# The first calls of the work beside a second alignment moved ahead: two before its second step, one past its fifth

## The reference

```python
x = x + _L0_xattn_ref(ctx_1024, _layernorm(x, axis=-1))   # an alignment (DTW) of 64 latents to 1601 rows
x = x + _L0_attn_ref(_layernorm(x, axis=-1), ...)         # a gated linear recurrence, 64 steps
x = x + _L0_ffn_ref(_layernorm(x, axis=-1), ...)          # 8 experts, top 2, and a shared one
```

```python
r = d_ij + jnp.minimum(jnp.minimum(up, left), diag)        # the table
...
choice = jnp.argmin(jnp.stack([cd, cu, cl]))               # the path, from its end
...
expanded = jnp.zeros((T_large, d), dtype=small.dtype).at[j_idx].add(contrib)
```

## Time and profile before

| | |
|---|---|
| median of three runs | 1174.21 us |
| the profiled execution | 1176.61 us |
| its span, first to last instruction | 1175.4 us |
| mean granted TensorE clock | 0.938 of full |
| busy: PE, DVE, ACT, POOL | 86%, 56%, 42%, 10% |
| chain that ended last: PE, DVE, DMA | 55%, 29%, 6% |

### The profile page before, as it was taken

The page is one execution under the profiler, slowest core; times in us unless marked ns, Lnnn a source line. Parts: engine busy times, 40 slices in busy tenths (PEclk is TensorE's granted clock), DMA queues, the critical chain, the costliest instruction groups (busy, mean ns, idle before and its releaser), DMA issues.

```text
span 1175.4 us, 15523 instructions
## 1 busy us (share of the span) xinstructions
PE 1005.5 (86%) x4892; PEld 598.2 (51%) x4892; DVE 660.5 (56%) x2311; ACT 494.2 (42%) x847; POOL 115.5 (10%) x150
## 2 busy tenths in 40 slices
PE   5886639888891799997899699887999999999998
PEld 2332213333330455553576465645676767676776
DVE  4994949999999776487669612427311111111116
ACT  4885627766781345423242155243222222222221
POOL 1000000000000000000000000000252425242210
PEclk9998979999996799988899799799999999999999
DMA  9999954565876989440050097394121212123115
GB/s 354 324 309 272 274 155 141 154 190 157 237 225 163 327 252 329 135 150 11 1 186 1 0 336 249 104 349 174 49 83 57 83 56 84 56 84 105 32 52 182
DMA packets 123806, 190.47 MB, mean 162 GB/s; under 512 B 9008, under 2 KB 93136, under 8 KB 123728
## 3 DMA queue, kind: packets, MB, share of 16 engines
q1 hardware_dynamic: 117840, 171.13, 47.0%
q0 software_dynamic: 5888, 18.36, 5.1%
HBM read 165.43 MB, written 24.03 MB: 161 GB/s over the span
## 4 chain that ended last, share of the span: by engine, by line
PE 55%; DVE 29%; DMA 6%; issue 4%; ACT 3%; SPq 2%; POOL 0%; DVEq 0%; ACTq 0%; POOLq 0%
PE bank L1816 13%; PE bank L1663 8%; PE bank L1847 7%; PE bank L1684 4%; DVE table L825 4%; PE bank L1808 3%; DMA spaced<-dist 3%; DVE beyond L841 3%; DVE passed L846 3%; PE bank L1827 3%; DVE col_min L818 2%; DVE z L756 2%; PE bank L1590 2%; PE bank L1839 2%; PE bank L1811 2%
## 5 line engine op out<-in xcount | busy, mean ns | idle before, releaser
L1028 DVE TENSOR_TENSOR hid<-bank,act_s 128x352 f32<-128x352 f32 x104 | 54.2, 524 | 220.9 <-PE bank L1816 182.1
L1816 PE MATMUL bank<-w_up,srcT 128*128 x512 | 162.9, 460 | 0.8 <-ACT srcT L1434 0.8
L1574 PE MATMUL bank<-sq,ones 128*64 128x402 f32 (+1 forms) x512 | 101.3, 517 | 38.2 <-ACT sq L1291 38.2
L1442 ACT ACTIVATE act_s<-bank 128x352 f32<-128x352 f32 x104 | 47.9, 463 | 198.4 <-PE bank L1816 127.7
L1816 PEld LDWEIGHTS bank<-w_up,srcT 128*128 128x128 f32 x512 | 96.0, 189 | 47.9 <-issue 4.1
L1590 PE MATMUL bank<-table,ident 128*128 128x402 f32 x144 | 68.5, 560 | 56.3 <-DVE stays L789 51.0
L1568 PE MATMUL bank<-ctxT,latT 128*64 128x402 f32 (+1 forms) x512 | 101.2, 517 | 4.8 <-DMA ctxT<-ctx_tr_dram 4.0
L1663 PE MATMUL bank<-rows_c,on_path 128*64 128x256 f32 (+1 forms) x832 | 100.8, 395 | 2.4 <-DMA rows_c<-ctx_nat_dram 1.6
L1291 ACT ACTIVATE sq<-ctxT 128x1608 f32<-128x1608 f32 x64 | 97.5, 1526 | 8.5 <-DMA ctxT<-ctx_tr_dram 8.5
L1847 PE MATMUL bank<-w_dn,hidT 128*128 (+1 forms) x384 | 93.6, 380 | 0.4 <-DVE y_sb L1042 0.4
L1328 ACT ACTIVATE code<-bank,unpassed 128x402 bf16<-128x402 f32 x72 | 42.1, 589 | 122.9 <-PE bank L1592 122.9
(11 more groups left out here) (292 smaller groups left out, 1619.5 us busy)
## 6 DMA issues: line engine op xcount, KB each, us to landing
rows_c<-ctx_nat_dram SPq DMA_DIRECT2D x32, 896.0 KB
ctxT<-ctx_tr_dram SPq DMA_DIRECT2D x32, 804.0 KB, 8.7
ctxT<-ctx_tr_dram SPq DMA_DIRECT2D x32, 797.0 KB, 7.5
rows_c<-ctx_nat_dram SPq DMA_DIRECT2D x32, 640.0 KB
spaced<-dist SPq DMA_DIRECT2D x128, 101.0 KB, 3.8
w_up<-w_t_dram SPq DMA_DIRECT2D x16, 704.0 KB, 13.3
table<-spaced SPq DMA_DIRECT2D x48, 202.0 KB, 4.2
w_dn<-w_t_dram SPq DMA_DIRECT2D x16, 256.0 KB, 5.8
```

The costliest lines, as they stand in the source:

```text
L1028: e.tensor_tensor(hid[i][:, :], psum[2 * i + 1][:, 0:HH], act_s[i][:, :], ALU.mult).then_inc(hid_done, 1)
L1574: last = e.matmul(ps[b * T:(b + 1) * T, 0:nq], ones[:, 0:T], sq[i][:, b, k, 0:nq], start=False, stop=(k == KC - 1))
L1816: last = e.matmul(psum[2 * i + m][:, 0:HH], srcT[t % 2][:, k, :], w_up[:, bass.ds(ex, 1), m, k, columns], start=(k == 0), stop=(k == KC - 1))
```

## The change

`behind_second` gave no calls in slots 0 to 5. It now gives two past slot 0 and one past slot 4. From slot 6 on it gives what it gave.

```diff
 def behind_second(n):
 
     if n < 6:
-        return 0
+
+        return {0: 2, 4: 1}.get(n, 0)
     if n < 33:
         return min((n - 6) % 4, 1)
     if n < CODE_SLOTS:
```

## The result

The change made the kernel slower by half a per cent: 1180.26 us in the median (1175.51 to 1183.41, 20 runs) against 1174.47 us (1170.08 to 1180.53, 20 runs), ratio 1.0045 with an interval from 1.0034 to 1.0056. Two later batches gave 1.0046 (1.0031 to 1.0061) and 1.0050 (1.0032 to 1.0067). The forecast was 1173.0 us, with a range up to 1178.5 us: time and sign were both wrong. One single execution of all, in the third batch's first kernel, took 5738.9 us; it stands apart from every other and is left out of that kernel's ratio. The profiled execution took 1180.26 us, its span is 1179.0 us, the mean granted clock 0.939.

The account below looks back on a forecast made before the run. TensorE bounds 410 to 514 us, neither engine 514 to 609 us, VectorE 609 to 664 us. A 6.4 us gain at recurrence 1's sums of squares, less 3.8 and 1.4 us, left 1.2 us: 1173.0 us, range 1168.5 to 1178.5 us.

Parts of the forecast that it names:

- Part 1: First pair: the first half of the sums starts at about 389.9 us, 4.7 us earlier, at half clock.
- part 2: First pair's second half: block lands at 397.1 us, full clock, 2.8 us; TensorE leads by 0.6 us at the second pair.
- part 3: VectorE's owed steps through recurrence 0, paid in its waits: recurrence 1 starts 3.0 us earlier, three steps short.
- Part 4: Chain of recurrence 1: second `kv` at 560 us, sums of squares at 564.4 us, 6.4 us earlier; owed steps fit before.
- Part 5: Back steps behind `lg`: four more remain, 3.8 us, plus 1.4 us of waits; second path terms come 1.2 us earlier.
- the sum: Whole kernel: 1.2 us earlier, from 1174.21 us to 1173.0 us in the median.
- Theory U: Experiments' theory, ahead of the moved part: early calls slow the last context rows' load; first path terms at 382 to 383 us.
- Halves ahead of gaps starve TensorE: Rival, 389.9 to 407 us: half-clock second half, late block, slow first gap, 5.1 us more, 1178 us; chance 0.2.
- More gain: Rival: owed steps paid in VectorE's idle time from 514 to 609 us, added gap hidden, 1170.6 us; chance 0.2.
- The change doesn't do what it says: Rival: block landings set everything and the three owed steps cancel the rest, no difference, 1174.2 us; chance 0.15.

Follow-up runs that it names:

- third batch's first kernel: The change with its three early calls given back at slots 33 to 35, against the kernel before: 1178.80 us, ratio 1.0032.
- given back at slot 7: The change with its three early calls given back at slots 7, 8 and 9: 1179.93 us, 1.0048; with fourth and fifth block loaded ahead of the weights: 1174.01 us, 0.9995.
- given back at slot 33: The change with three calls given back at slots 33 to 35: 1178.80 us, 1.0032; blocks ahead of the weights too: 1174.67 us, 0.9985, again 1174.08 us, 0.9991.
- one call ahead: The change with two of three calls given back, at slots 33 and 34: 1178.40 us, 1.0024; with blocks ahead of the weights too: 1175.12 us, 0.9994.
- blocks first: The change, with SP loading the fourth and fifth block of rows ahead of the six weights: 1175.93 us, ratio 1.0015 to before.
- three calls more: The kernel before, first pair unmoved, with no early call but three more calls at slots 33 to 35: 1183.28 us, ratio 1.0071.
- given back at 53: The change with its three calls given back only at slots 53, 54 and 56, past recurrence 0: 1186.03 us, ratio 1.0086 to before.
- four calls ahead: The kernel before, first pair unmoved, with four more calls at slots 33 to 36: 1185.59 us, ratio 1.0109.
- The kernels with both costs out: The change with calls given back at slots 33 to 35 and blocks loaded ahead of the weights: 1174.67 us, 0.9985; again 1174.08 us, 0.9991.
- The second version of the last batch: The change with two calls given back, at slots 33 and 34, and blocks loaded ahead of the weights: 1175.12 us, ratio 0.9994 to before.
- the other version of that batch: The change with three calls given back at slots 33 to 35 and blocks loaded ahead of the weights, run again: 1174.08 us, 0.9991.

## Why the prediction was wrong

**Part 1 held**: the products, the start of the first half and its clock. The 28 matmuls took 4.57 to 5.83 us, inside the 6.3 us allowed.

**The first step that failed is in part 2:** the lead of 0.6 us with which TensorE was to start the second pair. It was 2.7 us behind instead, 3.3 us worse. Two terms of it were sized wrongly. The block: the second half started 19.6 to 20.0 us behind the path terms, at 398.3 to 398.8 us by the forecast's time, past the value taken (397.1) and the bound set (398.0). TensorE stood still for 2.4 to 3.5 us where I had reckoned 0.9 us at most, since the first half took less than 6.3 us. The clock: the half was priced at 2.8 us, at full clock, and took 4.4 to 4.5 us in two of three profiles.

With the blocks loaded first and all else the same, the second half neither waits nor runs slow (2.81 us in all five such profiles), and the second pair starts 26.8 us behind the path terms: in equal work 0.8 us ahead of before, about the 0.6 us forecast. The time fell by 0.31% (1.0046 to 1.0015), 0.53% (given back at slot 7: 1.0048 to 0.9995), 0.47 and 0.41% (given back at slot 33: 1.0032 to 0.9985 and 0.9991) and 0.30% (one call ahead: 1.0024 to 0.9994), which is 3.5 to 6 us. From the path terms to the start of the second pair the profiles show 3.5, 4.2, 4.7 and 3.5 us of it. From path terms to path terms only 1.7 to 3.6 us are left; single executions differ by as much there, so where the rest went is open.

**The second step that failed is in part 3:** "As TensorE is the full engine until 514 us, the steps are paid in waits that VectorE has anyway", and "one gap less ahead of it, 1.6 us: 2.2 us earlier". Counted from the path terms, the last share of recurrence 0 came 2.2 us later, on the mean, and recurrence 1 started 1.3 us later instead of 3.0 us earlier. One gap less did stand ahead of the `w_o` product (21 instead of 22), but of those left, one had moved between the two `kv` products and one between the sums of squares and the `w_o` product. I had counted gaps per stretch and not looked between which two instructions of the chain each falls.

The runs show the sum of these moves. In the six profiles with the list three calls ahead there (three of the change, blocks first, three calls more, given back at 53) the wait for `val` is 3.12 us and sixth to eighth addition takes 36.9 to 39.8 us. In the fourteen others, level, one or four calls ahead, the wait is 1.45 us or none, and the additions take 33.4 to 35.7 us. The means differ by 4.1 us:

| stretch of recurrence 0 | six profiles | fourteen | difference |
|---|---|---|---|
| second last `kv` to last `kv` | 13.6 | 12.1 | +1.5 |
| last `kv` to its product with the gate (L961) | 3.7 | 2.9 | +0.8 |
| from there to the last share (L971) | 11.3 to 14.3, mean 13.1 | 9.9 to 12.1, mean 10.9 | +2.2 |
| last share to eighth addition | 8.8 | 9.2 (8.8 one ahead) | -0.4 |

So the gap between the sums and the `w_o` product is about half of it, the other gap and the comparison the rest. No run moves one of the three alone. The wait of 0.8 to 0.9 us for the store of `latents2` ahead of recurrence 1 is gone in all three profiles, as forecast. And an engine's idle time pays nothing that stands behind the waiting instruction: VectorE's waits for `decay` and `kv` were as long as before, and its last step forward ended 5.9 us later behind the path terms than before, on the mean.

**Part 4 held in its mechanism.** First to second `kv` took 9.3 us, as forecast, against 12.5 us. What failed is "the steps still owed and the two scans fit ahead of 564 us": a code subtraction and two back steps stood ahead of the mean squares. -2.7 us instead of -3.4 us.

**Part 5 held:** +5.2 us forecast and measured, with 54 back steps behind `lg` instead of 50, and 2.0, 2.0 and 0.9 us of idle time there against 0.3 us. The close match has some luck in it: half of 2.27 us for one or two calls is 1.1 or 2.3 us, not the 1.4 us taken, and the three readings are 60.07, 60.06 and 58.85 us. That it grows with the distance is shown: 54.4 us when level, 55.4 us one call ahead, 60 us three ahead, 63.6 us four ahead.

**Nothing ahead of the change was in the sum**, and it holds 2.8 us of the difference in profiles. Theory U, that early calls cause it, fell as a rule: of the twelve profiles of other kernels with early calls, nine show the usual 4.75 us at this unit, eight of them with both halves early, and three show 5.82, 6.01 and 7.69 us. But the five profiles without early calls all show 4.75 us, and all three of the change are late, by 0.7 to 3.3 us. Similar delays of up to 2.3 us came at the 56th unit, in before too (1.2 us). The kernels with both costs out keep both halves early and lose nothing, so early calls as such do not cost this time. Whether it is a property of the change's program or chance is not settled.

**The range.** The bounds were put together as -4 to +3 us. Simply added, they reach from 3.3 us below the sum to 8.3 us above it, 1169.7 to 1181.3 us, and the measured 1180.3 us lies inside.

**The rivals.** "Halves ahead of gaps starve TensorE" gave 1178 us, the nearest of all, and named the right place. Its late block was right (398.3 to 398.8 us for 398.0). Its half clock was right in two of three profiles, at 1.6 us instead of 2.7 us. Its slow first gap was not: the first gap behind the halves took 0.90 us for its first two matmuls. TensorE fell behind by 2.7 us instead of 4.5 us. The argument against it, that the pause is 0.9 us at most, failed with part 2. The rule of the Trainium skill ("TensorE: Matmul & The Clock Gate", "HAM oscillation — how this bites in real kernels") that bursts with DMA waits between them start at half clock is borne out in five of the six profiles in which the second half waited more than 2 us for its block: 4.17 to 4.50 us behind waits of 2.4 to 3.7 us, and 2.81 us behind 3.29 us in the sixth. In a seventh (given back at slot 7) it waited 2.13 us for its mask and took 4.50 us. "More gain" failed with part 3: it too spent idle time on steps that stood behind the wait. "The change doesn't do what it says" was right that the landing of the blocks sets the start, and had no loss in it.

## What to carry to other kernels

Where one list is interleaved with another, moving a few calls moves every later one. Read the order at each later chain and ask between which two of its instructions the filler now stands; a gap of 1.6 us in front of a wait shortened the wait by its own length; three pieces moved inside the chain cost 4.1 us. Count the idle time of an in-order engine as available only to work that stands in its list ahead of the wait. Work moved into a hole can lose more than it gains if its second input is queued behind other loads: here moving the loads first gave back 0.3 to 0.5%. And price a wait of TensorE with the clock behind it: here 1.6 us on top of the wait itself.

## What the runs showed of the hardware

The same program can run the same matmuls at either clock. The change's second half took 2.81 us behind a wait of 3.29 us (granted clock 1.00), 4.42 us behind 3.45 us (0.62) and 4.47 us behind 2.39 us (0.61).

Stretches whose lists are the same differ between executions in this way too. The second version of the last batch lost here, behind 664 us, what it had won. Timeline of TensorE in a later recurrence:

```profile
759.01 1.09 PE L1913 MATMUL bank<-ident,hn 128*128 128x128 f32 x8 [2.08 <-DVE hn L719]
...
761.98 3.62 PE L1686 MATMUL bank<-hT,w_r 128*128 128x512 f32 x4
```

and the same in the other version of that batch:

```profile
763.51 1.10 PE L1913 MATMUL bank<-ident,hn 128*128 128x128 f32 x8 [1.16 <-DVE hn L719]
...
766.18 1.88 PE L1686 MATMUL bank<-hT,w_r 128*128 128x512 f32 x4
```

The pause ahead was 2.08 us in place of 1.16 us, and four matmuls take 3.62 us at 1.2 GHz instead of 1.88 us at 2.4 GHz (granted clock 0.63 from 762 to 769 us, 1.00 in the other). Seven of the eighteen experiments' profiles took 511 to 514 us behind the second path terms, the rest 509.3 to 509.7 us.
